# A decoder of two layers on one core: the queries' rotary sums by accumulating DMAs on GpSimd instead of additions on VectorE, in new orders

## The chip, the cores and the metric

The kernel runs on one core of a Trainium2 chip. The number is the time of one execution on the device in microseconds, the median of several runs.

## The reference

Eight sequences of 256 tokens and 256 features pass two layers; after each of six blocks comes x = layernorm(x + block(x)).

```
L0 attn : layernorm, x @ W_in -> (xh, z); causal conv of 4 taps, silu; B, C, dt from xc @ W_xp;
          h_t = exp(dt A) h_(t-1) + dt B xc   (512 channels, 16 states, 256 steps);  y = sum_n C_n h_n + D xc
          out = (y * silu(z)) @ W_out + x
L0 xattn: cosine similarity of a visual and a text projection
L0 ffn  : 4 experts (rank-4 additions to one hidden layer of 1024, relu), the best 2 weighted
L1 attn : 16 query heads, 4 key heads of 64; rotary; softmax(q k / 8) v; output projection (low-rank parts)
          rotary: [x1 cos - x2 sin, x1 sin + x2 cos] with x1, x2 the even and odd features
L1 xattn: layernorms, one-head attention over the context
L1 ffn  : gated recurrence over the 8 sequences (forget, input, tanh), tanh output
```

## The kernel before, in words

All arithmetic is in f32. The work of a batch (one sequence) is cut into four streams of steps: F, the front of L0 attn up to the convolution and its projections; S, its scans; W, L0 xattn and L0 ffn (a part x) and L1 xattn and L1 ffn (a part z); Y, L1 attn. Every engine has a hand of generators, one per stream, and a string in ORDER whose letters say which stream's next step the engine gets. Within one engine all instructions run in this order, so the strings fix how streams and batches interleave; semaphores do the rest. In parts W, the x part of batch b stands ahead of the z part of batch b - 1.

**S.** A batch has 16 units (4 groups of states by 4 chunks of channels). Per unit ScalarE makes the decay (L495, L498), VectorE the input (L516), the scan (L520) and the product with C (L523). In batches 0 and 1 TensorE sums 4 states by products with the identity (L475). From batch 2 on GpSimd issues two accumulating DMAs, which fold four states into two (L547, 256 KB) and two into one (L552, which waits for the first), and TensorE adds the one left. There are three buffers for the decay, and ScalarE reuses one when TensorE has summed it. B and C rows (BC, 1 MB for a group of states) are loaded by SP.

**Y.** TensorE transposes x (a "turn"), projects keys (L288 with w_k), queries in four quarters n = 1 to 4 (L288 with w_q, 512 columns into one bank) and values (w_v). VectorE multiplies a quarter out of the bank with the cosines and, with halves swapped, with the sines: L1219 and L1220, written to rot, two tiles in ya. L1244 adds both into queries, two tiles in yo. TensorE transposes the sum (L1064) into a bank, ScalarE copies it to qT (L1176). Keys go the same way (L1237, L1238, L1054). A projection waits for the products of the quarter before, since there is one bank. Then 16 heads: scores (L1105), row maximum (VectorE L1259), exponential (ScalarE L1193), transposes (L1112), copy (L1200), values (L1123), scaling (L1184), and at the end transposes (L1143) and the output product (L1150). Batch b's Y needs its x part done, which needs its scans done.

**x and z.** In L0 ffn, L626 is the base product, L631 the experts' low-rank products, L716 the Relu, L798 the maximum added, L637 the transposes, L721 their copy, L671 the output. In z, L883 and L889 are the recurrence's products and L871 the transposed weights of its attention.

Of the kernel before, what the change touches and what calls it, by code (L numbers as in the profile page):

```python
# [13 lines left out]
P = 128  # L14
# [33 lines left out]
        "FFFFSFWWFWFSSYSFYSFYYSYWYSYYSYYSYYSYYSYYSSFSSFSFSFSSFSWWWSWSFWSFWWSWFSWSWWSWWWSWWFSWSWWFWWSWWSWFSWYFSYSYYYYYSY"  # L48
        "YSSYYSYFYWWYYWYWYYYWFYSYYSYYYWYYYWWFSYYYYYYYSYYSYYYWWSYYYWWYSYYWYYYWYYYWWYSYWYSYYYWWFSYYWYWSWYYWSYYWYSYYYYSFFW"
        "WYYYWYYWSYYWYYWFYSWYYFSSYSWYWYFWYWYWYYWYYWSYWYYYSYYFYWWYYWWYYSWYYYYYWYSYYSYYYFSWYYWYFWSYYYWYYWWYSWYYWFWYSYWYWF"  # L50
        "WSYYWYWWWSYYWYYWSYYWSYYFSFYWWYYYWYYWYYSWYYSWYSSWSYYWYYWYWWYWYYWSYWYYWSYYYFYWYYWWYYYWYYSWYSYWYYSYYYYSYYWYWYYYSW"
        "YYYWYYWWYWSYYWYYWSYWFWYYWSYWWFWYSWYYWSYWYYWYSYSFYWWFYYYWYYWYYYSWYYSWYFWSSYWYYWSYWYWYYWYWYYWYSWYYFSYYYWWWWYYYSW"
        "FYYYWSYYYSYYYWYSYYYWYYWYSYYFYYYFWYYSFWWYSWYWYYWYSYYWWYYWSYWWYWWSWYWYSWYSYFYSWWYYYYWYWYYYWYSYSSWYYWYYWSYFWYYWWY"
        "WYWYYSWYWYYSYYYFWYWWSYWYYYYWFYSYYWSYYYSYYWYWWYYYYYSYWYWYYWYWYWYYWYSYWWYFSWYYSWWFWYYWYYWSYWYWYYSSFYSWYWYYWYYWYY"
        "YWSYYWYFSWSSYWYYWSYWYWYYWYWYYWYWYYSYYYSYWWYYWWYYYWSYYYYWYYSYYSYYYYWYWWYYYSYYSWYYYWWYWYYWYYYWSYWWYYWSYWWYWWWWYS"
        "WYYSSWYWYYYWYYSWYYYWSYYWYWYYWSYYWWYWYWYSYSSWYYWYWYYYYYYWWYWYWYYYWYYWYYYYYYYWYWYYYWYYYWYYWYWYYWWYWYYWYWYYWYYWWY"
# [1545 lines left out]
```

## Time and profile before

| | |
|---|---|
| median of 3 runs | 1382.21 us (1398.91, 1377.51, 1382.21) |
| profiled execution | 1379.84 us, span 1377.9 us |
| TensorE, VectorE, ScalarE, GpSimd busy | 1160.8, 1056.9, 794.5, 290.7 us |
| granted clock of TensorE, mean of the span | 0.936 |
| scans of batch 7 (L520), first and last start | 1000.31, 1120.45 us |

Busy time of an engine is the union of its instructions. Matmul records are counted twice for a product in f32 (x32 for 16 products), except the transposes. A pause, below, is the time between the last scan of one batch and the first of the next.

### The profile page before, as it was taken

To read this page: it belongs to the slowest core of one execution; us is meant where nothing else is said; L and a number is where in the kernel's file an instruction comes from. 1 tells how busy PE (TensorE), PEld (TensorE's weight loads), DVE (VectorE), ACT (ScalarE), POOL (GpSimd) and SP (SyncE) were. 2 spreads that over 40 slices of the span, in tenths; PEclk is the share of its full clock that TensorE was granted. 3 is DMA by queue.
4 is the path that set the end of the run, shared out by engine and by line. 5 is a ranking of instruction groups with operands and counts; after the bars stand their busy time and mean duration, and the time that the engine had idled before them with its cause. 6 is when DMAs were issued, how large, how long until landed. Compare 5 with 4: busy or idle time off the path is not lost.

```text
span 1377.9 us, 16592 instructions
## 1 busy us (share of the span) xinstructions
PE 1160.8 (84%) x5760; PEld 921.4 (67%) x5760; DVE 1056.9 (77%) x1719; ACT 794.5 (58%) x1989; POOL 290.7 (21%) x341
## 2 busy tenths in 40 slices
PE   4697677888899799989998899988998989989852
PEld 2454456666678577866786678867786768868741
DVE  3998899899869797899879897998699763343216
ACT  3433545467658665677567756776477545536521
POOL 0000201222421333232313231324122420010001
PEclk9877999989999899999999999999999999999976
DMA  4612010234424424234414442533343320000301
GB/s 183 242 46 71 7 63 8 77 77 92 101 54 92 89 47 115 58 81 99 110 31 100 86 96 55 110 76 60 92 104 77 50 51 20 1 0 8 121 0 61
DMA packets 55285, 100.27 MB, mean 73 GB/s; under 512 B 5417, under 2 KB 28810, under 8 KB 54562
## 3 DMA queue, kind: packets, MB, share of 16 engines
q0 software_dynamic: 27648, 37.76, 16.8%
q1 hardware_dynamic: 27554, 61.46, 13.8%
q8 instruction: 45, 0.74, 0.2%
q14 instruction: 38, 0.31, 0.1%
HBM read 55.42 MB, written 6.04 MB: 45 GB/s over the span
## 4 chain that ended last, share of the span: by engine, by line
PE 40%; DVE 31%; DMA 9%; ACT 9%; issue 7%; POOL 4%; DVEq 0%; SPq 0%; ACTq 0%; POOLq 0%
PE bank L288 15%; DVE scans L520 10%; DMA scans<-scans 9%; PE bank L1105 4%; DVE scans L516 4%; DVE scans L523 4%; PE bank L1150 3%; PE bank L1123 3%; PE bank L475 2%; DVE nmax L1259 2%; DVE conv L399 2%; PE bank L671 2%; PE bank L883 2%; ACT scans L498 2%; PE bank L889 1%
## 5 line engine op out<-in xcount | busy, mean ns | idle before, releaser
L520 DVE TENSOR_TENSOR_SCAN scans<-scans 128x1024 f32<-128x1024 f32 x128 | 292.3, 2284 | 16.4 <-ACT scans L498 11.9
L498 ACT ACTIVATE scans<-dt,a_neg 128x255 f32<-128x255 f32 x512 | 221.4, 500 | 0.0
L475 PE MATMUL bank<-scans,ident 128*128 128x256 f32 x448 | 138.7, 432 | 49.9 <-DMA scans<-scans 27.0
L1193 ACT ACTIVATE ya<-bank,nmax 128x256 f32<-128x256 f32 x256 | 107.1, 472 | 86.1 <-DVE nmax L1259 86.0
L523 DVE TENSOR_TENSOR scans<-scans,BC 128x1024 f32<-128x1024 f32 x128 | 155.7, 1217 | 1.2
L1259 DVE TENSOR_REDUCE nmax<-bank 128x2 f32<-128x512 f32 x128 | 87.3, 683 | 90.2 <-PE bank L1105 89.1
L516 DVE TENSOR_TENSOR scans<-conv,BC 128x1024 f32<-128x1024 f32 x128 | 155.7, 1216 | 0.1
L552 POOL DMA_DIRECT2D scans<-scans x96 | 84.1, 876 | 289.1 <-DMA scans<-scans 287.8
L475 PEld LDWEIGHTS bank<-scans,ident 128*128 128x128 f32 x448 | 87.8, 210 | 85.5 <-DMA scans<-scans 38.9
L1123 PE MATMUL bank<-v,ya 128*128 128x65 f32 x1024 | 135.5, 278 | 4.4 <-ACT yo L1184 4.4
L1123 PEld LDWEIGHTS bank<-v,ya 128*128 128x128 f32 x1024 | 132.6, 201 | 8.3 <-issue 5.9
L547 POOL DMA_DIRECT2D scans<-scans x96 | 90.4, 941 | 187.5 <-DVE scans L523 186.2
L495 ACT ACTIVATE scans<-neghalf 128x4 f32<-128x4 f32 x128 | 26.9, 210 | 117.0 <-PE bank L475 116.7
L1105 PE MATMUL bank<-kzO,qT 128*128 128x256 f32 x256 | 74.1, 415 | 20.4 <-ACT ya L1200 20.4
L1200 ACT ACTIVATE ya<-bank 128x512 f32<-128x512 f32 x128 | 76.9, 601 | 14.4 <-PE bank L1112 14.3
L288 PE MATMUL bank<-xnT,w_in 128*128 128x256 f32 x256 | 72.8, 436 | 13.5 <-DVE zg L420 8.5
L1112 PE MATMUL bank<-ident,ya 128*128 128x128 f32 x512 | 81.0, 283 | 0.1
L1105 PE MATMUL bank<-kzE,qT 128*128 128x256 f32 x256 | 68.8, 391 | 13.9 <-ACT ya L1200 12.8
L1112 PEld LDWEIGHTS bank<-ident,ya 128*128 128x128 f32 x512 | 66.7, 147 | 15.0 <-issue 3.2
L288 PEld LDWEIGHTS bank<-xnT,w_in 128*128 128x128 f32 x256 | 55.2, 222 | 26.4 <-DVE zg L420 8.5
L1105 PEld LDWEIGHTS bank<-kzO,qT 128*128 128x128 f32 x256 | 48.4, 201 | 33.7 <-ACT ya L1200 26.7
L1184 ACT ACTIVATE yo<-bank,rs 128x64 f32<-128x64 f32 x256 | 59.7, 325 | 18.9 <-DVE rs L1252 18.8
(255 smaller groups left out, 2229.6 us busy)
## 6 DMA issues: line engine op xcount, KB each, us to landing
BC<-xpj_scratch SPq DMA_DIRECT2D x32, 1024.0 KB, 6.1
scans<-scans POOLq DMA_DIRECT2D x96, 256.0 KB, 3.4
scans<-scans POOLq DMA_DIRECT2D x96, 128.0 KB, 2.7
xin<-in_x SPq DMA_DIRECT2D x8, 256.0 KB, 4.3
conv<-in_x SPq DMA_DIRECT2D x8, 256.0 KB, 2.9
out<-scans SPq DMA_DIRECT2D x8, 256.0 KB, 2.7
kept_x<-x SPq DMA_DIRECT2D x7, 256.0 KB, 2.0
kept_w<-wa SPq DMA_DIRECT2D x7, 256.0 KB, 2.0
```

Source lines behind the costliest of these rows:

```text
L288: last = pe.matmul(o, l, r, start=(start and i == 0), stop=(i == n - 1), skip_group_check=True)
L475: last = pe.matmul(sums_of(c), ident[:, :], step_of(b, u)[:, i, :], start=False, stop=(h == UH - 1 and i == SUMMED[b] - 1), skip_group_che ...
L498: ins = act.activation(step[:, j, 1:S], dt[b % 2][:, c, 1:S], ACT.Exp, scale=a_neg[:, c, n:n + 1])
L516: dve.tensor_tensor(dBx, conv[b % 2][:, c:c + 1, :].to_broadcast([P, HN, S]), Bh, ALU.mult).then_inc(s["a_dBx"], 1)
L520: dve.tensor_tensor_scan(flat(H[:, :, :]), flat(H[:, :, :]), flat(dBx), 0.0, ALU.mult, ALU.add).then_inc(s["a_scan"], 1)
L523: dve.tensor_tensor(flat(H[:, :, :]), flat(H[:, :, :]), Ch, ALU.mult).then_inc(s["a_hC"], 1)
L547: pool.dma_start(flat(H[:, 0:2, :]), flat(H[:, 2:4, :]), accum_op=ALU.add).then_inc(SUM_OF[(NU * b + u) % 3], 16)
L1105: last = pe.matmul(YB[h % 2][:, t * S:(t + 1) * S], qT[:, pair, t * P:(t + 1) * P], kz, start=True, stop=True)
L1112: last = pe.transpose(YB[h % 2][:, k * S + t * P:k * S + (t + 1) * P], pe_[:, h % 2, t, k * P:(k + 1) * P], ident[:, :])
L1123: last = pe.matmul(y2[:, o:o + HD + 1], pT[:, h % 2, k, t * P:(t + 1) * P], v1[:, k, g, :], start=(k == 0), stop=(k == 1))
L1193: act.activation(pe_[:, h % 2, t, :], YB[h % 2][:, t * S:(t + 1) * S], ACT.Exp, bias=nmax[:, h % 4, t:t + 1]).then_inc(s["t_p"], 1)
L1259: dve.tensor_reduce(nmax[:, i % 4, :], YB[i % 2][:, :].rearrange("p (t k) -> p t k", t=T), AX, ALU.max, negate=True).then_inc(s["t_max"], 1)
```

## The change

y_dve no longer adds the two products. Instead y_pool issues, per quarter, a DMA that accumulates the sine products onto the cosine products in place (rot[n % 2], 128 partitions x 512, 256 KB). It waits for the products (t_rot) and for the landing of the quarter before (t_ro, now 16 per DMA). TensorE transposes rot instead of queries, and queries is gone. Products 3 and 4, which write rot anew, wait for the transposes of quarters 1 and 2 (t_qT_ps) instead of the sum. GpSimd gets four Y steps per batch. All five orders are laid anew. Lines of the new kernel are one lower than those of the old from L237 on (L1063 is the old L1064); L1270 is the new DMA.

```diff
-    t_kr=2, t_ro=4,
+    t_kr=2, t_ro=16 * 4,
@@ y_pe, turned_queries(n)
-                pe.wait_ge(*of("t_ro", b, n))
+                pe.wait_ge(*of("t_ro", b, 16 * n))
-                    last = pe.transpose([y1, y0][(n - 1) % 2][:, f * P:(f + 1) * P], queries[n % 2][:, f * P:(f + 1) * P], ident[:, :])
+                    last = pe.transpose([y1, y0][(n - 1) % 2][:, f * P:(f + 1) * P], rot[n % 2][:, 0, f * P:(f + 1) * P], ident[:, :])
@@ y_dve
-                    dve.wait_ge(*of("t_ro", b, n - 2))
+                    dve.wait_ge(*of("t_qT_ps", b, n - 2))
...
-                    dve.wait_ge(*of("t_rot", b, 4 + 2 * n))
-                    if n >= 3:
-                        dve.wait_ge(*of("t_qT_ps", b, n - 2))
-                    dve.tensor_tensor(queries[n % 2], rot[n % 2][:, 0, :], rot[n % 2][:, 1, :], ALU.add).then_inc(s["t_ro"], 1)
@@ y_pool
+            for n in range(1, 5):
+                pool.wait_ge(*of("t_rot", b, 4 + 2 * n))
+                if (b, n) > (0, 1):
+                    pool.wait_ge(*of("t_ro", b, 16 * (n - 1)))
+                pool.dma_start(rot[n % 2][:, 0, :], rot[n % 2][:, 1, :], accum_op=ALU.add).then_inc(s["t_ro"], 16)
+                yield
@@ ORDER, the last line of "pe" (one of 40)
-        "YWWYWYWYWYYYYYYYYYWYYWYYWYWYYWYYYYWYYYWYYYWYYYWYYYWYYYWYYYWYYYWYYYWYYYWYYYYYYYYYYYYWYYYWYYYYYYYYWWWWWWWWWWWWWW"
+        "WWWWWWWWWWYWYYYYYYWYYWYYWWYYWYYWYWYYYWYYWYYYYWYYYWYWYYYYYWYYYWYYYYYYYYYYYYWYYYWYYYYYYYYYYYYYYYYWWWWWWWWWWWWWW"
```

**TensorE, rotary part of batch 5, from the third projection of queries (w_q) on.** Before:

```order
L288 MATMUL bank<-w_q,yT 128x512 x2
L288 MATMUL bank<-cxT,wa 128x256 x4
L475 MATMUL bank<-scans,ident 128x256
L1064 MATMUL bank<-ident,yo 128x128 x4
L288 MATMUL bank<-w_q,yT 128x512 x2
L871 MATMUL bank<-ident,wa 128x128 x4
L1064 MATMUL bank<-ident,yo 128x128 x4
L288 MATMUL bank<-xnT,w_in 128x256 x4
L475 MATMUL bank<-scans,ident 128x256
L288 MATMUL bank<-wa 128x256 x4
L288 MATMUL bank<-w_out,zg 128x256 x8
L1064 MATMUL bank<-ident,yo 128x128 x4
```

The same place now:

```order
L287 MATMUL bank<-w_q,yT 128x512 x2
L474 MATMUL bank<-scans,ident 128x256
L1063 MATMUL bank<-ident,ya 128x128 x4
L287 MATMUL bank<-w_q,yT 128x512 x2
L870 MATMUL bank<-ident,wa 128x128 x4
L1063 MATMUL bank<-ident,ya 128x128 x4
L474 MATMUL bank<-scans,ident 128x256
L287 MATMUL bank<-wa 128x256 x4
L1063 MATMUL bank<-ident,ya 128x128 x4
```

The product of cxT between projection 3 and its turn, and the products of w_in and w_out between projection 4 and the last turn, now stand elsewhere: the turns of quarters 3 and 4 follow closer on their projections.

**TensorE, feed-forward of batch 7 after the last scan (L631, L626, L637; L1105, L1112 and L1123 are heads of batch 6).** Before:

```order
L631 MATMUL bank<-w_b,lowT 128x512
L637 MATMUL bank<-ident,wa 128x128 x4
L1105 MATMUL bank<-kzO,qT 128x256 x2
L626 MATMUL bank<-w_i,xT 128x512 x2
L631 MATMUL bank<-w_b,lowT 128x512
L1112 MATMUL bank<-ident,ya 128x128 x4
L1123 MATMUL bank<-v,ya 128x65 x4
L631 MATMUL bank<-w_b,lowT 128x512
L1112 MATMUL bank<-ident,ya 128x128 x4
L637 MATMUL bank<-ident,wa 128x128 x4
L1123 MATMUL bank<-v,ya 128x65 x8
```

The same place now, up to the output product:

```order
L630 MATMUL bank<-w_b,lowT 128x512 x3
L636 MATMUL bank<-ident,wa 128x128 x4
L625 MATMUL bank<-w_i,xT 128x512 x2
L630 MATMUL bank<-w_b,lowT 128x512 x2
L636 MATMUL bank<-ident,wa 128x128 x4
L625 MATMUL bank<-w_i,xT 128x512 x2
L630 MATMUL bank<-w_b,lowT 128x512 x2
L636 MATMUL bank<-ident,wa 128x128 x8
L670 MATMUL bank<-w_o,wa 128x256 x16
```

The heads of batch 6 stood between the feed-forward's steps; now they are over when it begins, and it stands alone.

**GpSimd, the same part of batch 5 (L1270 a rotary DMA; L546 and L551 the two folds of a unit).** Now:

```order
L1270 DMA ya<-ya 128x512
L551 DMA scans<-scans 128x256
L546 DMA scans<-scans 128x512
L551 DMA scans<-scans 128x256
L1270 DMA ya<-ya 128x512
L546 DMA scans<-scans 128x512
L1270 DMA ya<-ya 128x512
L551 DMA scans<-scans 128x256
L1270 DMA ya<-ya 128x512
```

Before, only the folds stood here. The second rotary DMA now stands behind a fold that waits for another to land.

## Rows read from the trace of the kernel before

**Rows 1.** The page: busy time and share of each engine; the chain by engine.

```profile
PE 1160.8 (84%) x5760; PEld 921.4 (67%) x5760; DVE 1056.9 (77%) x1719; ACT 794.5 (58%) x1989; POOL 290.7 (21%) x341
...
PE 40%; DVE 31%; DMA 9%; ACT 9%; issue 7%; POOL 4%; DVEq 0%; SPq 0%; ACTq 0%; POOLq 0%
```

**Rows 2.** Windows: two pauses, a scan stretch, the tail's start; first line names columns.

```profile
core 0: us, PE busy (x) PEld busy (x) DVE busy (x) ACT busy (x) POOL busy (x), PEclk, DMA share, GB/s
534.30:563.40 29.10, 28.76 (x134) 22.16 (x132) 19.39 (x45) 13.35 (x30) 7.18 (x9) 1.00 0.37 100
...
710.20:823.50 113.30, 99.81 (x528) 81.00 (x527) 104.15 (x151) 78.45 (x205) 33.33 (x39) 0.94 0.42 84
...
969.10:1000.30 31.20, 31.20 (x154) 25.23 (x153) 19.26 (x38) 16.33 (x38) 4.46 (x6) 1.00 0.26 61
1132.00:1215.00 83.00, 76.79 (x444) 65.57 (x443) 28.20 (x86) 41.22 (x106) 3.73 (x8) 0.98 0.03 9
```

**Rows 3.** Groups by line and shape: count, busy us, mean ns, idle before.

```profile
L1259 DVE TENSOR_REDUCE nmax<-bank 128x2 f32<-128x512 f32 x128 | 87.3, 683 | 90.2 <-PE bank L1105 89.1
...
L716 ACT ACTIVATE wa<-bank,sc 128x512 f32<-128x512 f32 x32 | 22.2, 697 | 12.3 <-PE bank L631 12.0
...
L1244 DVE TENSOR_TENSOR yo<-ya 128x512 f32<-128x512 f32 x32 | 22.1, 692 | 1.1
...
L798 DVE SCALAR_TENSOR_TENSOR wa<-bank,wa 128x512 f32<-128x512 f32 x32 | 21.5, 676 | 3.9 <-PE bank L631 3.8
```

**Rows 4.** Timeline, VectorE: one add of batch 5 (start, duration).

```profile
974.39 0.69 DVE L1244 TENSOR_TENSOR yo<-ya 128x512 f32<-128x512 f32 x1
```

**Rows 5.** Chain of waits from 534 to 564 us: start, duration, what.

```profile
550.43 7.16 PE bank L288 x28
```

**Rows 6.** Instructions on yo: who waited for VectorE's writes (us, times).

```profile
  PE bank L1064: 1.7, 2
```

**Rows 7.** Chain of waits in the tail, same columns.

```profile
1270.80 0.86 PE bank L1105 x4
1271.66 0.44 PE bank L1112 x4
1272.10 0.84 PE bank L1123 x8
...
1303.07 7.19 PE bank L1150 x32
```

**Rows 8.** Timeline of batch 7's rotary part: its turn, first add, first scores.

```profile
1215.19 1.11 PE L282 MATMUL bank<-ident,x 128*128 128x128 f32 x4 [2.83 <-ACT x L277]
...
1225.01 0.69 DVE L1244 TENSOR_TENSOR yo<-ya 128x512 f32<-128x512 f32 x1
...
1238.88 1.03 PE L1105 MATMUL bank<-kzE,qT 128*128 128x256 f32 x4
```

**Rows 9.** The page: L547's group; DMA issues with size and us to landing.

```profile
L547 POOL DMA_DIRECT2D scans<-scans x96 | 90.4, 941 | 187.5 <-DVE scans L523 186.2
...
BC<-xpj_scratch SPq DMA_DIRECT2D x32, 1024.0 KB, 6.1
scans<-scans POOLq DMA_DIRECT2D x96, 256.0 KB, 3.4
```

**Rows 10.** Timeline: a fold beside a BC load, one alone; then the wait summed.

```profile
972.17 0.36 SPq L452 DMA_DIRECT2D BC<-xpj_scratch  x1
...
972.44 0.88 POOL L547 DMA_DIRECT2D scans<-scans  x1 [6.32 <-DVE scans L523]
...
979.96 0.87 POOL L552 DMA_DIRECT2D scans<-scans  x1 [6.64 <-DMA scans<-scans]
...
1124.98 0.90 POOL L547 DMA_DIRECT2D scans<-scans  x1 [2.26 <-DVE scans L523]
...
1128.77 0.86 POOL L552 DMA_DIRECT2D scans<-scans  x1 [2.89 <-DMA scans<-scans]
...
POOL scans L552 <- DMA scans<-scans: 287.8, 82, 8.4
```

More of the change, by code:

```diff
@@ L47 @@
     "pe": (
[L48 to L56, printed above, removed]
@@ new lines @@
+        "YFWWYWYWYYSWYWYSWYYWYWWSWYWYYSYFSYYYYYYWSYYWYYSFYYYYYFSYYWYWSYYWSSWYYWYWYYSWYFWWWWWWYSYYFYWWWWYYSWYFYSYYWFYYYS"
+        "YYYWYWSYYWYYYFYWSYWYYWYYWWYSYYWYYYWWFYYYWSYYYWWSFYYYWSWYYYWYWYYSWYYSYYSYYYYWYWSYYYWYYWYSWYYSWYYWSSYYWYYWSYWYYW"
+        "WYYYWWYYWYYYYYSFYYWWYYWWYYSSWYYYWFYYYFYYFYYWYYWYWYSYYYWYWSWWYYWYWYWSWYYYWYWWYSWWWWYYWYYSFYYYYSWSYWSYYWYYWYSWYY"
+        "YSYYWYSWYWYYWYWWWWSWYYWYSYSSYYYWYSYYYWWYWYYYWYYYWYYYSYYYWWYYYSWYYWYSWWYWYYYYYWYWYYYYYSWYWYYSWYYSWWYYWWYYYYSWWW"
+        "SYYYYYSSYYWYYSWYYWWYSWYYYWWYSYYYSWYYWYYYWYSYYYWYYYSWYYSYYYSYYYYWWYYWYYYYYYYWWYYYWYYYWYYYWYYWYYYWYYWYYYYWWWWWWW"
@@ new lines @@
+        "WSWYSYYSSYSYSYYWYYWSSFFWWFYYWWYYWYYWWYSSSSYWWSYSSWFWWWYSSYYFWFWSYYSWSFYYYWSYYSSYYYSSWYYWFWYYYSSYYWFWYWYSYSYWYF"
+        "WWYYYSWSYYWSSYYWSSYSSYYWFSSYYYYWYWYYFSYYWFSYYWWYWYWWYYSSFWSSYYWFFWSSFWWWYSSYYSFWWYWSSYYFWSYYYSFYYSSWYYWYSYYWYS"
+        "YYFWSWYYWYYWYSSYYSWFYYYWFYYWSSYYYSWSYYWSSYYYYYSYYYYSSSWSSWWYYWWWYYWYYWWYYYWYWYSYFWSSSYYSSWSYYYWYYWSYYYFYYWFWFY"
+        "WYYSSSWSSYYFYYFYYYWFWYYYWYYSWYYWYWSSWYYWSSYYWYYSWWWYSSYYYYSFSWWSWSSSYYSSWWWYWYSYYSSSYWWYYWYWYYWWWYYWYYYWYYSSYW"
+        "YSYWSSYYSSWYYYYYSWSYWYYWYYSSWYYYWSWSYYYYWYYYYWYYWYSSYSSWYYSWYYSWSSYSSWYWYYSSSWSSYSYWWWWYYSSYWWYYYSSYYWYYWYYYYY"
@@ L80 @@
+        "SFSSSWWFSSSYSSSWYYSSSSYSSYSWYSWSSWSYSYYWWSYSSYYYYSYSWSSYYWYSSYSYSWYWWWYSYSSSYSWYWYSSYSSYSYWYSSSWSSSSSSYSSWWWSS"
+        "SYYSYSSYSSYSSSSWSWYYSWYSSSYSYYSYYYSWYYYSYYWYYYYYYYYYWWYWWWWYWWWWWWWYYYYYWWYYWYYYYYYYYWYYWYYYWYYYYYYYYYYWWWWWWW"
         "WWWWW"
@@ L100 @@
     f_z1_ps=4, f_z2_ps=4, f_r1=4, f_h=4, f_hT_ps=4, f_hT=4, f_out_ps=1, f_res=1, f1_norm=T,
-    t_xT_ps=1, t_xT=1, t_proj_ps=5, t_rot=12, t_kr=2, t_ro=4, t_v_ps=1, t_v=1, t_kT_ps=2, t_kz=4, t_qT_ps=4, t_qT=4,
+    t_xT_ps=1, t_xT=1, t_proj_ps=5, t_rot=12, t_kr=2, t_ro=16 * 4, t_v_ps=1, t_v=1, t_kT_ps=2, t_kz=4, t_qT_ps=4, t_qT=4,
     t_s_ps=NQ, t_max=NQ, t_p=2 * NQ, t_pT_ps=NQ, t_pT=NQ, t_o_ps=NQ, t_rs=NQ // 2, t_o=2 * NQ, t_oT_ps=4, t_oT=4, t_out_ps=1, t_var=1, t_rstd=1,
@@ L236, in build @@
         keys = yo[:, 0:3, :].rearrange("p a s -> p (a s)")[:, 0:T * (NKV + 1) * HD].rearrange("p (t n) -> p t n", t=T)
-        queries = [yo[:, 3 + 2 * i:5 + 2 * i, :].rearrange("p a s -> p (a s)") for i in range(2)]
         ob = yo[:, :, :].rearrange("p (t a) (h d) -> p t (a h) d", t=T, d=HD)
```

42 lines of the change are left out of this document (20 added, 22 removed).

## The prediction

> **What bounds the kernel now.** I read the page's busy shares and its chain of waits first [rows 1]: TensorE is busy 84% of the span, VectorE 77%, and the chain that ends last runs 40% on TensorE, 31% on VectorE and 9% on the folding DMAs. No engine is the bound by itself, so I cut the span at the scans. The scans of one batch are 16 units; between the last scan of a batch and the first of the next lies a pause, in which the front of the next batch, attention and the rotary part run. The windows [rows 2] show two kinds of stretch. In a pause TensorE never rests (28.76 of 29.10 us, 31.20 of 31.20), and VectorE is busy 19 of 29 to 31 us. In a scan stretch it is the other way: VectorE 104.15 of 113.30 us (92%), TensorE 88%. After the last scan comes a tail of 250 us on batch 7, whose first 83 us have TensorE busy 76.8 [rows 2]. So an edit is worth what it takes off VectorE in a scan stretch, off TensorE in a pause, and off the chain in the tail.
>
> **What is removed.** 32 additions of 0.692 us, 22.1 us [rows 3]. 28 of them stand before the last scan, 19.4 us. Where do they stand? One of batch 5, in the pause from 969 to 1000, is at 974.39 [rows 4], and TensorE's chain of that kind of pause is a row of products with nothing of VectorE between them: 7.16 us of L288 in one piece [rows 5]. In the orders of VectorE, batches 1 to 5 have their rotary part within one unit of this pause in both kernels. The cover of the adds is TensorE's full pause, and they are worth nothing there; if that cover went, they would be worth their whole time. What TensorE waited for the adds is 1.7 us [rows 6]: minus 1.7. In the scan stretches, the work that VectorE's order holds between first and last scan of a batch, each row at its duration from the grouped view, is 711.5 us over batches 2 to 7 before and 709.9 now: minus 1.6. All that is left over falls in the pauses. VectorE as a whole has 28 adds less and three row maxima more (0.683 us, [rows 3]) before the last scan: 19.4 - 2.0 = 17.4 us less. The sum above gives it 1.6; the chain share of VectorE, 31%, would give 5.4. A pause is not TensorE's to the last piece (it rests 0.34 us in the first one shown, and starts each scan stretch only when VectorE does), so I take the 5.4, 3.8 more than the stretches give. Its ends are 0 and 17.4.
>
> **What is moved.** Up to the last scan sum TensorE has four heads more in its order, scores, turns and values, and one group of gate products less. By the pieces of the chain [rows 7]: four heads at 0.86 + 0.44 + 0.84 us are 8.6, less 1.80 for the gate group (a quarter of L1150's 7.19): 6.8 us of work more before the last scan and 6.8 less after it. In the scan stretches this costs nothing (TensorE rests 12% of them). In the pauses, TensorE's work between the last sum of one batch and the first of the next is 133.4 us over the five pauses before batches 3 to 7 in the old order and 137.5 in the new: plus 4.1.
>
> **The tail.** 6.8 us less work. But the four heads were the filler of batch 7's feed-forward: before, heads stand between its products; now eight rows of it stand bare (second piece of order). I walk this chain: base products (1.8 each, as a quarter of L1150's 7.19), loras, and per hidden quarter a Relu (0.697), a maximum (0.676) [rows 3], a turn (0.44 [rows 7]) and a copy as long as the Relu; bare it takes some 13 us for 10.2 us of work, so 3 are given back. Then the rotary part of batch 7: from the turn at 1215.19 to the first scores at 1238.88 it took 23.7 us [rows 8]. With DMAs it is one chain: the first products are done at 1225.0, where the first add began [rows 8], then four DMAs one behind the other, since GpSimd issues each only when the one before has landed: 1225.2 + 4 x 3.8 = 1240.4, last turn and copy 1.1, scores at 1241.6. That is 2.7 later, of which 2.0 is work of the cross-attention that now stands ahead of the scores instead of behind: plus 0.7. Tail: -6.8 + 3.0 + 0.7 = -3.1.
>
> **What is added.** 32 accumulating DMAs of 128x512 on GpSimd. The same shape is in the trace: the first fold of each scan unit, 256 KB, issued in 0.94 us and landed after a median of 3.4 us [rows 9]; from its issue to the next instruction that waits for it is 3.79 us where nothing else moves [rows 10]. GpSimd's issue time, 32 x 0.94 = 30 us, lies in an engine busy 21% [rows 1] and costs only what it delays. For TensorE the delay from projection to turn grows from two products and an add (0.69 each) to 1.4 + 3.8 = 5.2 us, so I counted, for each of the 32 turns in the new order, the TensorE work that stands between projection and turn. It is 5.2 us or more in 26 of them. The six others lack 0.9 (batch 2), 2.2 and 2.2 (batch 5, first piece of order: 3.0 us of work each), 0.4 (batch 6), 0.4 and 1.3 (batch 7): 7.4 us, of which the 1.7 of batch 7 are in the tail's sum already. Plus 5.7. The lower end is 0 (TensorE's work runs somewhat behind the order's bare sum), the upper is the rival below. VectorE has a new wait too: products 3 and 4 wait for the turns of sums 1 and 2, and a scan's multiply can be queued behind them. TensorE has turn 1 ahead of projection 3, and turn 2 ahead of projection 4, in both orders, so the products could not start earlier anyway: nothing, except that a late DMA now holds the projection as well. GpSimd's waits: in batch 5 the second rotary DMA stands behind L551 (L552 before), which waits for a fold (last piece of order). Behind a rotary DMA, in turn, stands a fold; the wait for t_rot and the one for the DMA before can hold it, and TensorE's sum, ScalarE's next decay (three buffers) and the scan wait for that. Four per batch, in the pause, where folds have ended or not begun: I cost it at nothing, since GpSimd is busy 4.5 to 8.2 us of a pause [rows 2]; up to 3.8 per batch if not.
>
> Against this stands the Trainium skill, "DMA: Bandwidth & Descriptors", section on the anatomy of one DMA, SWDGE path: it fits a DMA at 2.0 us plus bytes over 436 GB/s, 2.6 us for this size, and then only some 2 us of the 5.7 would be left and the sum be 3.5 us lower. The trace has 3.4 for the landing of just this operation, and goes before it.
>
> **Sum.** -1.7 - 5.4 + 4.1 - 3.1 + 5.7 = -0.4 us. The profiled execution took 1379.84 us, so 1379.4, told as **1380 us**. The median of the three runs shown is 1382.21, 2.4 above the profiled one and within their scatter (1377.51 to 1398.91). I expect no difference that a measurement of this kernel can tell, which is about 2%, or 27.6 us.
>
> **Rival 1, VectorE's relief counts in full (0.22).** If the pauses follow VectorE, 17.4 goes instead of 5.4, the 4.1 in the pauses is not paid, and TensorE hides the DMAs: -1.7 - 17.4 - 3.1 = -22, 1358 us. For it: the planner's order reaches the last scan with four heads more done. Against: TensorE at 31.20 of 31.20 in the pause. With good luck in the waits it passes 1354.6, the 2% mark.
>
> **Rival 2, slower: the accumulations meet the BC loads (0.22).** In every pause SP loads 1 MB of B and C rows for the next scans. A fold beside it, issued at 972.44 with the load at 972.17, held its follower until 979.96: 7.52 us instead of 3.79 [rows 10]. The mean wait of L552 for a fold is 287.8 / 82 = 3.5 us [rows 10] where the undisturbed one is 2.9, so most folds are spared; but the load falls in the rotary part. A rotary DMA caught so is 3.7 late, the next is issued that much later, and TensorE's pause has no slack for it. The point from which it decides: a turn has less than 8.9 us of work ahead of it, and 17 of the 24 in batches 1 to 6 have. One DMA per batch for batches 1 to 6 is 22 us, 1402 us; two per batch, or with folds held up behind them on GpSimd at 3.8 a batch, 1425. Against: the load lasts 6.1 us [rows 9] of a rotary part of over 20. The Trainium skill, same page, section on issuing engines that are not separate queues, says that DMAs of all engines interleave on the same 16 DMA engines; by that rule, the trace agrees.
>
> **Rival 3, the change doesn't take work off (0.06).** The orders were laid for another balance and some stretch starves, in either direction, by up to 15 us around 1380.
>
> My forecast has the remaining 0.50, with a range of its own of 1366 to 1394. For 8 in 10 I reach to 1358 at one end and 1407 at the other. Faster than 1354.6: 0.10, from rival 1. Slower than 1409.9: 0.13, from rival 2's second half and a little of the measurement. Within: 0.77.
>
> **What would show it.** Right: VectorE's busy sum falls from 1056.9 by some 22 us and its share of the time falls with it; the last scan still ends between 1115 and 1130; the pauses still show TensorE above 95%; L1063 waits for the accumulating DMA some 4 to 10 us in all; the tail is 3 us shorter. Rival 1 shows as a last scan before 1110. Rival 2 shows as landings of the rotary DMAs with a median above 5 us and over 15 us of TensorE's waits for them. I would be wrong if GpSimd's folds got later on average: then ScalarE's wait for the sums (L495) would grow, and the scans wait inside their stretches.

## The result and the profile after

The changed kernel took **1421.64 us** (median of 4 runs, 1419.52 to 1421.78), the kernel before 1381.72 beside it: ratio 1.030, interval [1.0277, 1.0324]. It is slower by 3%, where I had forecast 1380 us and no difference.

The page of the changed kernel, answering to [rows 1] (busy time by engine; the chain that ended last), and its groups and DMA issues, answering to [rows 3, 9]:

```profile
PE 1183.2 (83%) x5760; PEld 931.0 (66%) x5760; DVE 1039.8 (73%) x1687; ACT 791.0 (56%) x1989; POOL 316.6 (22%) x373
...
PE 42%; DVE 30%; ACT 11%; DMA 8%; issue 7%; POOL 3%; DVEq 0%; SPq 0%; ACTq 0%; POOLq 0%
...
L1254 DVE TENSOR_REDUCE nmax<-bank 128x2 f32<-128x512 f32 x128 | 87.4, 684 | 91.5 <-PE bank L1104 90.9
...
scans<-scans POOLq DMA_DIRECT2D x96, 256.0 KB, 3.4
...
ya<-ya POOLq DMA_DIRECT2D x32, 256.0 KB, 3.3
```

VectorE did lose its additions (1056.9 to 1039.8 us of busy time), and the new DMAs land as fast as the folds do. Neither explains 40 us. The 32 new DMAs and who waited for them (the view of one line; its engine's idle time, then its waiters, in us and times):

```profile
L1270 POOL DMA_DIRECT2D ya<-ya x32: 859/872/1172, 245.7 to 1270.2; - x32
its engine sat idle before it (us, times) until:
  DVE ya L1219: 75.7, 20
  DMA ya<-ya: 23.5, 10
who waited for it (us, times):
  POOL ya L1270: 23.5, 10
  PEld bank L1063: 6.5, 9
  PE bank L1063: 3.4, 7
  POOL scans L546: 1.2, 1
```

TensorE's matmuls stood 3.4 us for them and its weight loads 6.5, mostly at the same moments (PEld waits beside PE, so the two aren't added, as e3's expectation below does when it says 9.9); one fold stood 1.2. So I cut the span at the scans again. Windows of the changed kernel, in the columns of [rows 2]: three pauses (before batches 4, 6 and 7), the scan stretches of batches 4, 5 and 6, and the first 83 us behind the last sum.

```profile
523.40:555.00 31.60, 29.09 (x124) 22.24 (x125) 16.27 (x40) 13.35 (x31) 9.06 (x14) 0.95 0.39 86
833.70:870.40 36.70, 34.66 (x165) 26.85 (x164) 21.22 (x52) 19.33 (x46) 10.18 (x13) 1.00 0.46 107
999.70:1034.40 34.70, 31.56 (x166) 27.28 (x166) 10.84 (x21) 16.65 (x41) 5.22 (x6) 0.95 0.30 87
555.00:681.90 126.90, 107.35 (x551) 87.63 (x550) 106.77 (x152) 83.86 (x218) 37.03 (x40) 0.92 0.41 79
718.00:833.70 115.70, 105.18 (x583) 85.83 (x581) 106.40 (x155) 83.62 (x216) 38.54 (x42) 1.00 0.43 82
870.40:999.70 129.30, 117.32 (x609) 92.08 (x607) 113.43 (x175) 85.44 (x219) 41.29 (x46) 0.97 0.43 81
1165.00:1248.00 83.00, 70.55 (x382) 57.77 (x381) 26.25 (x82) 36.54 (x91) 3.91 (x8) 0.98 0.03 9
```

Batch 4's stretch in the kernel before, same columns:

```profile
563.43:676.30 112.87, 100.41 (x547) 80.84 (x546) 105.40 (x153) 82.50 (x215) 33.76 (x38) 0.98 0.41 83
```

The reader is to see VectorE: in batch 4's stretch it has 106.8 us of work in 126.9 (84%), where it had 105.4 in 112.9 (93%) before. By the first and last scan of each batch on the timelines, the kernel after is 8.4 us ahead at the first scan of batch 4 (555.0 against 563.4), loses 14.0 in that stretch (126.9 against 112.9), 14.7 in batch 6's (129.3 against 114.6), 0.9 in those of batches 5 and 7 together, 11.4 in the three pauses between them, where TensorE is no longer full (34.66 of 36.70, 31.56 of 34.70), and 9.7 in the tail. The last sum starts at 1165.05 instead of 1132.66.

### The profile page after: what moved, and what is told of

It is laid out like the page before. It is cut to its first block, busy times and chain, and to the rows that moved or that the text cites. A ratio compares the mean times of both kernels' runs of the same rounds, so it can differ in the third digit from the quotient of the medians.

```text
span 1420.0 us, 16610 instructions
## 1 busy us (share of the span) xinstructions
PE 1183.2 (83%) x5760; PEld 931.0 (66%) x5760; DVE 1039.8 (73%) x1687; ACT 791.0 (56%) x1989; POOL 316.6 (22%) x373
## 4 chain that ended last, share of the span: by engine, by line
PE 42%; DVE 30%; ACT 11%; DMA 8%; issue 7%; POOL 3%; DVEq 0%; SPq 0%; ACTq 0%; POOLq 0%
PE bank L287 13%; DVE scans L519 9%; DMA scans<-scans 6%; PE bank L1104 5%; DVE scans L522 4%; DVE scans L515 4%; PE bank L474 3%; PE bank L1149 3%; PE bank L1122 3%; ACT scans L497 2%; PE bank L670 2%; PE bank L888 2%; PE bank L882 2%; DVE nmax L1254 2%; PE bank L1111 2%
## 5 line engine op out<-in xcount | busy, mean ns | idle before, releaser
L474 PE MATMUL bank<-scans,ident 128*128 128x256 f32 x448 | 142.8, 445 | 52.2 <-DVE scans L522 27.4
L1254 DVE TENSOR_REDUCE nmax<-bank 128x2 f32<-128x512 f32 x128 | 87.4, 684 | 91.5 <-PE bank L1104 90.9
L551 POOL DMA_DIRECT2D scans<-scans x96 | 85.5, 890 | 273.9 <-DMA scans<-scans 273.5
L474 PEld LDWEIGHTS bank<-scans,ident 128*128 128x128 f32 x448 | 89.9, 217 | 83.2 <-DVE scans L522 36.1
L1122 PE MATMUL bank<-v,ya 128*128 128x65 f32 x1024 | 132.2, 274 | 4.3 <-ACT yo L1183 4.0
L546 POOL DMA_DIRECT2D scans<-scans x96 | 89.5, 933 | 179.6 <-DVE scans L522 175.3
L1104 PE MATMUL bank<-kzE,qT 128*128 128x256 f32 x256 | 72.4, 407 | 14.7 <-ACT ya L1199 12.7
L494 ACT ACTIVATE scans<-neghalf 128x4 f32<-128x4 f32 x128 | 27.0, 211 | 96.7 <-PE bank L474 96.6
L1104 PE MATMUL bank<-kzO,qT 128*128 128x256 f32 x256 | 70.4, 398 | 11.3 <-ACT ya L1199 11.2
L1104 PEld LDWEIGHTS bank<-kzE,qT 128*128 128x128 f32 x256 | 48.0, 198 | 29.3 <-ACT ya L1199 19.6
```

The source lines that it names most:

```text
L474: last = pe.matmul(sums_of(c), ident[:, :], step_of(b, u)[:, i, :], start=False, stop=(h == UH - 1 and i == SUMMED[b] - 1), skip_group_che ...
L546: pool.dma_start(flat(H[:, 0:2, :]), flat(H[:, 2:4, :]), accum_op=ALU.add).then_inc(SUM_OF[(NU * b + u) % 3], 16)
L1104: last = pe.matmul(YB[h % 2][:, t * S:(t + 1) * S], qT[:, pair, t * P:(t + 1) * P], kz, start=True, stop=True)
L1122: last = pe.matmul(y2[:, o:o + HD + 1], pT[:, h % 2, k, t * P:(t + 1) * P], v1[:, k, g, :], start=(k == 0), stop=(k == 1))
L1254: dve.tensor_reduce(nmax[:, i % 4, :], YB[i % 2][:, :].rearrange("p (t k) -> p t k", t=T), AX, ALU.max, negate=True).then_inc(s["t_max"], 1)
```

## The experiments

All ratios are to the kernel before, run beside each on the same chip; one thousandth is 1.4 us. "Old" and "new" orders are the tables of the kernels before and after. For the time line, **stretch** is from the start of a batch's first scan to the end of its last, **pause** the time from there to the next batch's first scan, **tail** from the last sum to VectorE's last instruction.

### Orders and sum apart: e1 to e4

e1: the changed code, every engine in its old order, GpSimd's old one with 32 steps put in where the additions had begun. e2: the code before (additions) in the new orders. e3 and e4: no rotary sum at all, in new and in old orders.

```
e1:  ORDER of before;  "pool": old order + 32 rotary steps, each where an addition began
e2:  ORDER of after, without the 32 rotary steps of "pool";  code of before
e3, e4:
-                pe.wait_ge(*of("t_ro", b, 16 * n))
+                pe.wait_ge(*of("t_rot", b, 4 + 2 * n))
-                pool.dma_start(rot[n % 2][:, 0, :], rot[n % 2][:, 1, :], accum_op=ALU.add).then_inc(s["t_ro"], 16)
e3:  ORDER of after      e4:  ORDER of before      (both without the 32 rotary steps)
```

> The accumulating DMAs in the old orders of TensorE, VectorE, ScalarE and SP; GpSimd's old order with the 32 rotary DMAs put where the additions began in the trace of before. Theory 'the new orders cost' (the loss of 40 us lies in how the streams are laid, not in the DMAs): the turns wait some 1 to 3 us each where they stand close behind their projections, so 1382 to 1400 us, well below the changed kernel's 1421. Rival 'the DMAs cost' (GpSimd's queue and late sums hold up folds and turns whatever the order): 1415 or more.

> The old code with the additions on VectorE, in all five new orders (GpSimd's without its 32 rotary steps). Theory 'the new orders cost': 1415 to 1430 us, as slow as the changed kernel although no DMA is added. Rival 'the DMAs cost': 1375 to 1395 us.

> The new orders with neither addition nor DMA: the rotary sum of the queries is left out, TensorE transposes the cosine products alone. Theory 'the new orders cost': 1408 to 1420 us, since the changed kernel's waits for the rotary DMAs are only 9.9 us in its profile. Rival 'the DMAs cost': below 1385 us.

> The old orders with neither addition nor DMA: the rotary sum of the queries is left out. It prices the additions where they stood. By the prediction's step they are covered by TensorE's full pause: 1372 to 1382 us. If VectorE's relief counted in full, 1360 us or less.

| | VectorE's additions | DMAs | no sum |
|---|---|---|---|
| old orders | 1 (the kernel before) | e1 1424.02, 1.030 [1.0236, 1.0363] | e4 1383.95, 0.9998 [0.9968, 1.0028] |
| new orders | e2 1424.52, 1.0291 [1.0239, 1.0342] | 1.030 (the kernel after) | e3 1414.46, 1.0224 [1.0174, 1.0274] |

Three things follow. The additions cost nothing that can be told in the old orders: leaving them out gains 0.0002, in an interval of 0.3% (4 us) to either side. The new orders cost 30 us with no rotary sum in the kernel at all (e3 against e4); that is three quarters of the loss. And the DMAs cost 7 to 10 us in the orders laid for them (by the medians and by the ratios) but 40 in the old ones, where I had expected 1382 to 1400 us; there the rival, 1415 or more, was right. The view of waits in e1 (us in all, times, longest), L1063 being the turns that wait for the sums:

```profile
PEld bank L1063 <- DMA ya<-ya: 35.3, 16, 4.4
...
PE bank L1063 <- DMA ya<-ya: 29.6, 14, 4.2
```

A DMA put where the addition stood is late for TensorE in 16 of the 32 turns, by some 2 us each (35.3 us of weight loads' waits against the 6.5 of the kernel after). The new orders do solve that problem. What they cost elsewhere is the question.

### Where in the orders: hybrids h1 to h6

A hybrid takes each engine's steps from one table up to a point that all five have reached together, and from there the other table's sequence over the steps that are left. The rotary sum is left out in all.

```
order[e] = first[e][:cut[e]] + (second[e], without as many steps of each stream as first[e][:cut[e]] holds)
h1: new, then old before the scans of batch 4     cut: pe 374, act 367, dve 375, pool 89, sp 43
h2: old, then new before the scans of batch 4     cut: pe 373, act 366, dve 373, pool 89, sp 43
h3: old, then new behind the last sum             cut: pe 922, act 876, dve 801, pool 252, sp 83
h4: new, then old behind the last sum             cut: pe 938, act 889, dve 809, pool 252, sp 83
h5: new, then old before the scans of batch 5     cut: pe 510, act 494, dve 482, pool 130, sp 54
h6: new, then old before the scans of batch 7     cut: pe 796, act 760, dve 702, pool 212, sp 79
```

> The rotary sum is left out, as in the runs e3 (new orders, 1414.5) and e4 (old orders, 1384.0). Here every engine follows the new orders until just before the scans of batch 4 begin, and from there the old orders over the steps that are left. In e3 those scans began at 551.0, in e4 at 567.1. If the 30 us are lost by the new orders of batches 4 to 7 (a stretch of scans of 126 us against 113 twice, and the work behind the last sum), this run keeps the lead of the first half and takes the old second half: 1368 to 1384. If the lead is only work that was put off (work of other streams left for later), the second half pays for it and it lands at 1384 to 1400. If the loss were in the first half, it would be 1400 or more.

> The rotary sum is left out. The reverse: old orders until just before the scans of batch 4, new ones from there. If the new orders of batches 4 to 7 lose the time: 1414 to 1430 (all the loss, without the lead of the first half). If the loss is in the first half: about 1384. If it is spread over both: about 1400.

> The rotary sum is left out. Old orders until the last sum of the scans, the new ones only for the work behind it. What is left there is the same work in both, so only the sequence of the tail is priced. If the longer tail of e3 (253.5 us against 240.1) comes of its sequence, this run stands 5 to 13 us above e4's 1384.0; if it comes of work that the new orders left over for it, it stands within 4 us of it.

> The rotary sum is left out. New orders until the last sum of the scans, the old ones for the work behind it. If the tail's length comes of its sequence, 1402 to 1410; if it comes of the work left over, within 4 us of e3's 1414.5.

> The rotary sum is left out. New orders until just before the scans of batch 5, old ones from there. Against h1, which leaves the new orders one batch earlier (1375.35), this run has the new stretch of batch 4 as well. If that stretch costs what its length says (126 us against 112 from the same start): 1385 to 1391. If what it lacks is given back by the work it did more of: 1375 to 1380.

> The rotary sum is left out. New orders until just before the scans of batch 7, old ones from there. Batch 6's new stretch is 7 us longer than the old one and batch 7's 4 us shorter, with more work of the other streams in the former. If the longer stretch buys work for later, this run stands within 5 us of h5; if it is loss like batch 4's, 8 to 15 us above h5, near 1400. Leaving the new orders behind the last sum gave 1405.7.

| new orders are used | median us | ratio | interval |
|---|---|---|---|
| never (e4) | 1383.95 | 0.9998 | [0.9968, 1.0028] |
| until batch 4's scans (h1) | 1375.35 | 0.9949 | [0.9917, 0.9981] |
| until batch 5's (h5) | 1401.72 | 1.0137 | [1.0104, 1.0170] |
| until batch 7's (h6) | 1400.59 | 1.0116 | [1.0084, 1.0149] |
| until the last sum (h4) | 1405.74 | 1.0189 | [1.0133, 1.0245] |
| throughout (e3) | 1414.46 | 1.0224 | [1.0174, 1.0274] |

The new orders are good up to batch 4: 7 us better than the old (0.0049, with intervals that touch; w1 below says the same). All of the loss is made behind that point: 0.0275, 38 us, from h1 to e3. The rung from batch 4's scans to batch 5's is the highest, 26 us (0.0188), more than I had expected of h5 (1385 to 1391). Batch 7's stretch and the tail cost some 15 together (0.0108); the intervals of h4 overlap both neighbours, so they are not told apart. The two halves the other way round (h2, 1425.32, 1.0317 [1.0272, 1.0362]) agree: without the first half's gain the second half costs 32. h3 (1407.18, 1.0173 [1.0119, 1.0226]) came out 23 us above e4, where I had expected 5 to 13 or nothing; but it lays the tail's sequence over a remainder that it was not laid for, and 15 of the 23 stand ahead of batch 7's rotary turn (97.8 us from the last sum to it, 82.5 in e4). So I trust h4's 0.0035 (5 us) and the tails of the timelines (253.5 us in e3, 244.0 in h4, 240.2 in h1).

**What a rung holds.** The timelines of h5 and h1 (the two profiled executions differ by 32.8 us, h1's being the quickest of its runs) show 15 us in batch 4's stretch (127.1 against 112.3) and 17 in the pause behind it (51.3 against 33.9). The first is the new order's own. The second belongs to the splice: in the new stretch TensorE's order has 63 attention steps instead of 70 and 37 of stream W instead of 40, and the old sequence, as soon as it takes over, does what was put off before the next scan can start (183 matmul records in that pause; 164 in h1). e3, with the same stretch, goes on in the new order and has a pause of 34.3 us (142 records). So of the 26 us, **batch 4's stretch itself shows 14 to 15**; the others I take for the price of work put off, which h5 pays at once; no run tells the two apart further.

By the same reading, h6 as good as h5 does not make batches 5 and 6 free. From batch 5's first scan to batch 7's h6 takes 310.2 us and h5 294.7, but h6 comes to the former 15.5 us earlier, without h5's long pause, and both reach the latter at 1024.4. I had expected h6 within 5 us of h5 if batch 6's longer stretch bought work for later. It came so, but not for that reason: batch 7's stretch did not get shorter (123.6 us against 120.9). e3 beside h1 tells how it adds up in one order: e3 is 1.1 us behind at the first scan of batch 4, 15.5 at batch 5's, 24.3 at batch 6's, 36.2 at batch 7's, 32.2 at the last scan and 45.4 at the end.

h1 and e3 reach that stretch with the same steps done, at 550.0 and 551.0 us. The windows, h1 first, columns as above:

```profile
550.00:662.30 112.30, 100.28 (x546) 80.99 (x546) 105.30 (x153) 82.38 (x215) 34.42 (x38) 0.98 0.41 83
```

```profile
551.00:677.40 126.40, 105.68 (x551) 85.90 (x550) 106.85 (x153) 83.75 (x218) 36.66 (x39) 0.93 0.39 76
```

As many instructions to within five on every engine, though not all the same ones (64 matmul records of scores against 57, 21 of the output product against 32), and 14 us more. VectorE, ScalarE and GpSimd have 1.4 to 2.2 us more to do, TensorE 5.4, at a mean clock of 0.93 instead of 0.98; VectorE rests 19.6 us instead of 7.0. What TensorE's sum step L474 waited for in these two windows (the view of waits), h1 first:

```profile
PEld bank L474 <- DMA scans<-scans: 4.2, 5, 1.8
...
PE bank L474 <- DMA scans<-scans: 2.0, 2, 1.4
```

```profile
PEld bank L474 <- DMA scans<-scans: 13.1, 5, 4.5
PE bank L474 <- DMA scans<-scans: 11.6, 4, 4.3
```

TensorE stands 9 us more for folds, and VectorE 12.6 us more for others. The scans' starts in that stretch, from its first: 0, 5.8, 14.1, 20.5, 25.8, **34.2**, 44.8 in h1; 0, 4.7, 12.4, 19.6, 33.4, **44.8**, 50.1 in e3. The two part at the fifth and sixth scan, where e3 falls 10.6 us behind. Half of it is back at the seventh (5.3), and behind a third wait for a fold, 3.20 us at 623.86, it grows to 16.1 at the eleventh; at the last scan it is 14.0. The timeline of e3 at the first of these places (start, duration, in brackets the idle time before and what ended it):

```profile
581.64 1.22 PE L474 MATMUL bank<-scans,ident 128*128 128x256 f32 x2 [4.35 <-DMA scans<-scans]
...
582.65 1.71 PE L603 MATMUL bank<-ones,wa 128*128 128x1 f32 x8
582.90 0.21 ACT L494 ACTIVATE scans<-neghalf 128x4 f32<-128x4 f32 x1 [5.82 <-PE bank L474]
...
584.40 0.16 DVE L742 TENSOR_SCALAR ss<-bank 128x4 f32<-128x4 f32 x1 [5.38 <-PE bank L603]
...
584.48 2.29 DVE L519 TENSOR_TENSOR_SCAN scans<-scans 128x1024 f32<-128x1024 f32 x1
584.64 2.95 POOL L815 TENSOR_TENSOR rn<-ss,neghalf 128x4 f32<-128x4 f32 x1 [7.88 <-DVE ss L742]
...
587.57 0.92 POOL L551 DMA_DIRECT2D scans<-scans  x1
```

And h1's, the same instructions:

```profile
581.49 0.60 PE L474 MATMUL bank<-scans,ident 128*128 128x256 f32 x2
...
581.92 0.95 PE L603 MATMUL bank<-ones,wa 128*128 128x1 f32 x8
581.98 0.88 POOL L551 DMA_DIRECT2D scans<-scans  x1 [6.79 <-DMA scans<-scans]
582.12 0.21 ACT L494 ACTIVATE scans<-neghalf 128x4 f32<-128x4 f32 x1 [0.64 <-PE bank L474]
...
584.05 0.15 DVE L742 TENSOR_SCALAR ss<-bank 128x4 f32<-128x4 f32 x1
584.12 2.28 DVE L519 TENSOR_TENSOR_SCAN scans<-scans 128x1024 f32<-128x1024 f32 x1
584.28 2.94 POOL L815 TENSOR_TENSOR rn<-ss,neghalf 128x4 f32<-128x4 f32 x1 [0.53 <-DVE ss L742]
...
587.20 0.90 POOL L551 DMA_DIRECT2D scans<-scans  x1
```

In h1 TensorE has attention work until the fold is there, and by 584 VectorE is at its sixth scan. In e3 it has none left, all four engines stand behind one late fold, and VectorE is at its fifth: a unit of scans behind.

### Four guesses at the mechanism: k1, b1 and b2, f1 and f2, c1 and c2

k1 takes the knot of that timeline apart: L603 goes ahead of the sum steps, in batches 4, 5 and 6.

```
"pe" of after:   batch 4   S W  ->  W S        batch 5   S W  ->  W S        batch 6   S S W  ->  W S S
```

> The rotary sum is left out; new orders as in e3 (1414.5), with one kind of step moved on TensorE: in batches 4, 5 and 6 the step of L603 (the recombination's sums of squares) goes ahead of the sum steps L474 that stand before it, three places in all. In e3's batch 4 TensorE waited 4.35 us at L474 for a fold, L603 stood behind it, VectorE waited 5.38 us at L742 for L603 with a scan behind it, and GpSimd waited 7.88 us at L815 for L742 with a second fold behind it. If this knot is what makes the stretch of batch 4 last 126 us where the old orders have 113, most of it goes: stretch 116 to 119, time 1404 to 1409. If the late fold itself sets the pace (the next scan waits for the bank that it frees), under 3 us are gained.

1415.31 us, 1.0243 [1.0194, 1.0292]: nothing gained. The fifth scan came at 27.9 instead of 33.4 us, the sixth at 46.3 instead of 44.8: VectorE then stood 5.76 us at L1254 for scores of TensorE, which had waited 2.91 us for ScalarE. The expectation that the knot is the cause is refuted; with it untied, the late fold holds the next scan by another way: ScalarE stood 5.62 us for the sum L474 before it came to what TensorE needed.

b1 and b2 shrink the loads of B and C for the second half of each batch's units, beside which the slowest folds stand.

```
+                rows = HN if h < 2 else 1
-                sp.dma_start(BC[:, h % 2, :, :], ... [:, h * HN:(h + 1) * HN, :]
+                sp.dma_start(BC[:, h % 2, :, 0:rows * S], ... [:, h * HN:h * HN + rows, :]
```

> The rotary sum is left out; new orders as in e3 (1414.5). The second and third quarter's... that is, the loads of B and C for units 8 to 15 of each batch (two of four) carry 1 of their 8 rows, 128 KB in place of 1 MB, so units 8 to 15 use old values of B and C; all waits stay. Two of the three folds of a batch that take 7 to 8.5 us stand beside these loads. If the new orders lose their 30 us because they leave less room behind those folds, they gain much more here than the old orders do: 1385 to 1400, and the difference between new and old falls under 15 us. If the loads have no part in it, new and old both move by the same few us and the difference stays 25 to 32 us.

> The same small loads of B and C (units 8 to 15 use old values), rotary sum left out, old orders as in e4 (1384.0). The old orders' folds beside the loads end behind other work of TensorE (5.8 and 4.1 us of waits for folds in batch 6's stretch): 1376 to 1384 in both cases. Small loads tell something only as the difference from the new orders with the same loads.

1412.14 us, 1.0204 [1.0154, 1.0253] in the new orders, 1375.21, 0.9938 [0.9904, 0.9972] in the old. The loads cost 2 to 3 us in the one and 8 in the other; the difference between the orders grew to 37. So the loads are not what makes the new orders slower.

f1 and f2 take the folds away, and with them their latency.

```
-                pool.dma_start(flat(H[:, 0:2, :]), flat(H[:, 2:4, :]), accum_op=ALU.add)...
-                pool.dma_start(H[:, 0, :], H[:, 1, :], accum_op=ALU.add)...
-                    pe.wait_ge(*of_sum(b, u, ADDS[SUMMED[b]]))
+                pe.wait_ge(*of("a_hC", b, u + 1))
```

> Rotary sum left out, new orders as in e3, and GpSimd issues no folding transfers: TensorE sums what it reads without them as soon as VectorE's product is there (three of four states, in batches with one fold one of two, are left out of the sums; the steps stay in the orders, empty). If the new orders lose their 30 us to the folds' latency, new and old differ by under 12 us here. If they lose it to the sequence of VectorE, ScalarE and TensorE themselves, the difference stays above 20 us. Time of this one: 1365 to 1405.

> The same without folds in the old orders (e4: 1384.0). TensorE waits for folds for 27 us in all in the kernel before, some of it covered: 1360 to 1380.

1389.93 us, 1.0051 [1.0020, 1.0083] new; 1368.97, 0.9873 [0.9815, 0.9931] old. The difference is 25 us by the ratios (0.0178) and 21 by the medians, where e3 and e4 have 31 (0.0226) and 30.5: 6 to 10 us of the loss hang on the folds' latency. They hang where they should: batch 4's stretch falls from 126.4 to 116.2 us, 3.4 above the old order's without folds (112.8 in f2) instead of 14:

```profile
544.10:660.30 116.20, 101.67 (x551) 82.76 (x550) 106.45 (x152) 83.56 (x218) 10.40 (x9) 0.97 0.10 35
```

but the tail stays 12 us longer than the old one (253.4 against 241.3), and batch 6's stretch nearly as it was (124.8; 126.2 in e3). Both theories had their say: "under 12 us" is refuted, and "above 20" holds with a part missing.

c1 and c2 ask what the granted clock adds. In e3 it falls towards its lower level (0.50, 1.2 of 2.4 GHz) behind each of three long waits for folds in batch 4 (0.55 over 6 us, 0.73 and 0.50 over 3 us), and stands there for most of the time from 1325 to 1365 us in the tail. c1 was to fill those three waits, c2 the tail's, with matmuls that nobody reads (in c1 they add a constant to the sums).

```
c1:
+                for _ in range({(4, 2): 16, (4, 4): 11, (4, 7): 12}.get((b, u), 0)):
+                    pe.matmul(sums_of(c), ident[:, :], w_in[:, 0, 0:S], start=False, stop=False, ...)
c2, batch 7 alone: 2 ahead of each turn of heads 10 to 15, 4 ahead of the turns of the output, 3 ahead of its product,
and ahead of the waits for c_norm 30, c_xT 4, c_q 4, c_p 8, c_pT 3:
+                pe.matmul(SA[1][:, 0:S], ident[:, :], w_in[:, 0, 0:S], start=True, stop=True)
```

> Rotary sum left out, new orders as in e3 (1414.5). Three waits of TensorE for folds in batch 4 (4.35 us at unit 2, 3.0 at unit 4, 3.2 at unit 7), each followed by a granted clock of 0.50 to 0.82 over the next 3 to 6 us, are filled with 16, 11 and 12 matmuls on a constant tile (they add to the sums, whose values are wrong by it). If the low clock behind the waits lengthens the stretch, it is 3 to 5 us shorter (126 to about 122) and the granted clock stays at 1.00 there: 1408 to 1412. If the clock is only a companion, nothing is gained, or the fillers cost their own time: 1414 to 1418.

> Rotary sum left out, new orders as in e3. Batch 7 alone has matmuls that nobody reads ahead of TensorE's waits in the tail: 2 before each turn of the last six heads, 4 and 3 around the output product, 30 before the wait of 7.8 us for the normalised rows, and 4, 4, 8 and 3 in the cross-attention. In e3 the granted clock from 1325 us on is 0.50 for most of 45 us, and the output product L1149 takes 9.64 us there. If the clock makes the new orders' tail long (253.5 us against 240.1 of e4), the tail falls by 6 to 12 us: 1402 to 1409. If the tail is bound by VectorE and ScalarE anyway, under 3 us: 1412 to 1417.

c1: 1421.83 us, 1.0254 [1.0195, 1.0312]; c2: 1417.68, 1.0235 [1.0170, 1.0300]. No gain in either. The windows show the clock held up where a wait was filled. First e3, then c1, at the first filled wait and behind it (here the columns are us, PE busy, clock, DMA share, GB/s):

```profile
576.00:582.00 6.00, 1.65 (x14) 0.88 0.97 230
582.00:588.00 6.00, 6.00 (x22) 0.55 0.01 2
```

```profile
576.00:582.00 6.00, 5.53 (x32) 1.00 0.56 194
582.00:588.00 6.00, 6.00 (x33) 1.00 0.26 47
```

The clock stayed up, and the fifth scan still came at 34.5 us (33.4 in e3). But the fillers were no clean test. TensorE's timeline of c1:

```profile
578.90 7.12 PE L470 MATMUL bank<-w_in,ident 128*128 128x256 f32 x32
...
585.86 0.59 PE L476 MATMUL bank<-scans,ident 128*128 128x256 f32 x2
...
627.50 1.22 PE L476 MATMUL bank<-scans,ident 128*128 128x256 f32 x2 [3.18 <-DMA scans<-scans]
...
640.92 5.40 PE L470 MATMUL bank<-w_in,ident 128*128 128x256 f32 x24
```

The first fold was issued at 577.01 and landed 6.3 us later, at 583.3; the filler ran past it, so its sum came 2.5 us late. From the sum to the fifth scan it then took 1.50 us instead of e3's 2.84: what the clock gave back, the filler had used up. The third filler stands ahead of unit 7, which had no wait; the wait of unit 6 stayed (3.18 us, the clock 0.50 over the 3 us behind it), and the filler's 5.40 us came on top. The stretch is 135.1 us long. c1 leaves open what the clock costs there.

In the tail, 1325 to 1370 us, all columns, e3 and c2:

```profile
1325.00:1370.00 45.00, 28.99 (x88) 21.21 (x88) 6.14 (x23) 9.45 (x21) 2.67 (x6) 0.62 0.00 0
```

```profile
1325.00:1370.00 45.00, 44.75 (x234) 39.45 (x234) 5.09 (x18) 11.60 (x29) 1.78 (x4) 1.00 0.00 1
```

From 0.62 to 1.00, and the tail was 251.4 us instead of 253.5. Here too a filler ran over: the 30 ahead of c_norm ended at 1356.36, and ScalarE had written what TensorE waited for by 1351.3, 5 us earlier. From the turn that stands there to VectorE's last instruction c2 took 55.7 us, its fillers included, and e3 61.2. And the tail can be priced without c2. From the start of the output product (L1149) to VectorE's last instruction, h1 and e3 do the same work:

```profile
1291.80:1363.21 71.41, 34.58 (x132) 26.50 (x132) 30.00 (x81) 14.28 (x25) 8.17 (x8) 0.74 0.05 17
```

```profile
1329.91:1408.52 78.61, 40.18 (x132) 30.29 (x132) 30.01 (x81) 14.28 (x25) 8.17 (x8) 0.67 0.05 16
```

The same instructions, the same busy time on VectorE, ScalarE and GpSimd; only TensorE's is longer (L1149 9.64 us against 7.17, the product of cxT and wa 3.78 against 1.99), and so is the piece, by 7.2 us. That is more than half of what e3's tail has over h1's (13.3), and it is the clock's. It is no constant of the new order: the kernel after takes 75.6 us for the piece and e2 73.2. How the orders come to it is argued, not tested: in h1 a product of 1.94 us (w_vo) stands in the last wait ahead of the output's turns and the clock stays at 1.00; e3 has done it earlier, TensorE is busy 3.10 of the 5 us up to 1325, and over the next 5 the clock is 0.50.

### A kernel better than both: w1

The code before, with its additions, in the orders of h1.

```
ORDER: new until just before the scans of batch 4, then old (cuts as in h1);  code of before
```

> The code before, with VectorE's adds, under the orders of the hybrid h1 (new until just before the scans of batch 4, old from there; without the rotary sum it took 1375.35, ratio 0.995). If adds cost nothing under old orders (e4 against before) and about 10 us under new ones (e2 against e3), three of eight batches are under new orders here: 1376 to 1383, within 1% of before and perhaps under it.

**1373.10 us** (1366.37 to 1377.18, 9 runs), 0.9917 [0.9891, 0.9943]: 11 us better than the kernel before, 3.7% under the changed one by the two ratios, and as good as h1, which has no rotary sum. I had expected 1376 to 1383. So additions on VectorE are free in these orders too; they cost 9 us (e2 against e3) only where the stretches already wait. It takes nothing of the change but the first half of its orders.

## Why the prediction was wrong, step by step

- **What is moved** is the step that failed. I weighed the new orders by sums of work: what stands between last and first scan, with TensorE's sums by pauses. That gave 4.1 us, and "in the scan stretches this costs nothing (TensorE rests 12% of them)". The runs show 30 us for the orders alone (e3 against e4), 14 of them in batch 4's stretch (126.4 us against 112.3), with as many instructions in it to within five. TensorE's 12% of rest says how much more it could do, not whether it has work at the moment when a fold is late. The sums of work were right (VectorE 106.85 us in that stretch against 105.30) and told nothing.
- **The tail** is the second: -3.1 forecast, +9.7 in the kernel after. By the timelines 2.4 stand before batch 7's rotary turn (82.5 us from the last sum to it before, 84.9 now; forecast -3.8, the 6.8 us less work and the 3.0 given back), 1.7 from the turn to the first scores (23.7, now 25.4; forecast +0.7), 1.4 in the heads and 4.2 from the output product on (71.4, now 75.6). The last is the same work at a granted clock of 0.68 instead of 0.74, a term that the forecast did not have.
- **What is removed**: VectorE's busy time fell by 17.1 us (I had said some 22), and none of it was worth anything, as the cover argument said and e4 shows (0.9998). The 5.4 that I took for the chain share of VectorE was against that argument and wrong. Rival 1 falls with it.
- **What is added**: +5.7 forecast, 7 measured by the medians and 10 by the ratios (the kernel after against e3), and TensorE's waits for them 3.4 (matmuls) and 6.5 us (weight loads), where I had named 4 to 10. This step was right in the main, landing time included (3.3 us). It holds in these orders alone: e1 shows 40.
- **Rival 2** (the DMAs meet the loads of B and C) is refuted: median landing 3.3 us, and small loads save 2 to 3 us in the new orders.
- **Rival 3** named the right cause, a stretch that starves because the orders were laid for another balance, with 0.06 and a bound of 15 us taken from nothing in the trace. A longer chain of four engines with three buffers could have been bounded from a timeline, as an estimate: one unit of scans lost per late fold, 5 to 8 us each by the distances of h1's scans.
- The signs: the last scan ended at 1155.3, where I had named 1115 to 1130, and TensorE filled 91 to 94% of the pauses shown, where I had named more than 95. The sign that I named for being wrong, L494's wait (L495 before) growing, did not come in the sum (116.7, now 96.6 us), but it came in batch 4's stretch: 19.0 us instead of 10.3, with VectorE's busy share down from 93% to 84%.

Shown: the orders make three quarters of the loss; all of it is made from batch 4's first scan on, 14 us in that stretch, where TensorE's waits for folds are 9 us longer, and where the orders differ by 3.4 us once the folds are gone; in e3's tail 7.2 of 13.3 us are TensorE's lower clock over the same instructions. Shown in part: over the whole span the folds' latency carries 6 to 10 of 30 us. Open: what in the sequence leaves TensorE without work when a fold is late, since untying the knot at L603 and small loads changed nothing; what the clock costs inside the stretches; and which waits make batch 6's stretch and the pauses longer.

## What to carry to other kernels

A change that comes with newly laid static orders is two changes: run the old code in the new orders, and the new orders without the disputed work, before judging the idea. Splicing two orders at points that all engines have reached together finds the region that costs, and here a splice beat both kernels; but a splice also pays at its joint for what the first order had put off, so the pause behind the joint has to be read before a stretch is charged. These in-order queues lost time not by the amount of work between two milestones but by who had something to do when a 3 to 7 us transfer was late; an engine that is 88% busy gives no cover by being 12% idle. And a DMA can replace an instruction of an idle-enough engine only if its consumer is moved later by the difference in latency: in the old place it cost 40 us, in a laid one 7 to 10, and the instruction it replaced had cost none. And a filler that is longer than its wait hides what it was to show: look at where its last matmul stands before reading the time.
